# Decoder kernel: a prefetch hint at the loop heads, GpSimd's waits placed later in its chain, softplus work inside the attention tails, and the second attention's start in another order

## What is computed

```python
x = x + delta_rule(ln(x))      # L0_attn: 2 heads of 128, chunks of 64; decay per token and head
x = x + quantum_attn(ln(x), ctx)   # L0_xattn: 16 heads of 16, q, k, v through tanh(x W1 + b1) W2 + b2
x = x + moe4_top2(ln(x))       # L0_ffn: 4 experts of 512, layer norm inside, relu
x = x + latent_attn(ln(x))     # L1_attn: one latent of 128; k and v shared by 16 heads; causal
x = x + cross_attn(ln(x), ctx) # L1_xattn: 16 heads of 16, causal
x = x + moe8_top2(ln(x))       # L1_ffn: 8 experts of 128, gelu
```

```python
log_decay = -exp(A_log) * softplus(ln(x) @ W_alpha.T + dt_bias)
cum = cumsum(log_decay within a chunk);  L_mask = tril(exp(cum_i - cum_j))
```

## Time and profile before

| | before |
|---|---|
| PE busy | 4795.6 us (82%) |
| DVE busy | 4255.7 us (73%) |
| POOL busy | 3819.3 us (66%) |
| ACT busy | 2318.7 us (40%) |
| mean granted TensorE clock | 0.937 of 2.4 GHz |
| chain that ended last | PE 48%, DVE 22%, POOL 13%, issue 9%, ACT 6% |
| one round (start of the round's first L934 to the next one's: 2387.41 to 2729.33) | 341.9 us |

### The profile page before, as it was taken

The page is one execution under the profiler, slowest core; times in us unless marked ns, Lnnn a source line. Parts: engine busy times, 40 slices in busy tenths (PEclk is TensorE's granted clock), DMA queues, the critical chain, the costliest instruction groups (busy, mean ns, idle before and its releaser), DMA issues.

```text
span 5816.3 us, 105933 instructions
## 1 busy us (share of the span) xinstructions
PE 4795.6 (82%) x28362; PEld 3131.5 (54%) x28362; DVE 4255.7 (73%) x11558; ACT 2318.7 (40%) x4416; POOL 3819.3 (66%) x10625
## 2 busy tenths in 40 slices
PE   1068888988888888888988888898888889888888
PEld 0045654656555465655646565564656556465654
DVE  5867677777777677776767768777776777777677
ACT  0034344444434444343444434344443444443344
POOL 1157585775767677576766758676675867767585
PEclk7589999999999999999999999999999999999999
DMA  3000000000000000000000000000000000000000
GB/s 83 7 12 8 20 1 17 12 9 20 1 27 1 12 16 8 20 1 23 5 8 20 9 20 1 23 5 8 20 8 20 1 24 5 8 20 6 15 1 16
DMA packets 61954, 78.93 MB, mean 14 GB/s; under 512 B 11168, under 2 KB 53808, under 8 KB 61232
## 3 DMA queue, kind: packets, MB, share of 16 engines
q1 hardware_dynamic: 52784, 62.42, 3.2%
q10 hardware_dynamic: 8448, 8.39, 0.4%
HBM read 45.04 MB, written 8.46 MB: 9 GB/s over the span
## 4 chain that ended last, share of the span: by engine, by line
PE 48%; DVE 22%; POOL 13%; issue 9%; ACT 6%; POOLq 1%; SPq 1%; DMA 0%; DVEq 0%; ACTq 0%
PE bank L1161 7%; POOL acc_c L567 4%; PE bank L1066 4%; PE bank L1080 4%; PE bank L1194 4%; PE bank L1280 4%; POOL arena L567 3%; PE bank L1092 3%; PE bank L990 3%; PE bank L997 2%; PE bank L1114 2%; PE bank L1179 2%; ACT arena L761 1%; POOL sl_t L567 1%; DVE arena L1906 1%
## 5 line engine op out<-in xcount | busy, mean ns | idle before, releaser
L1765 DVE TENSOR_REDUCE smax<-bank 128x4 f32<-128x512 f32 x768 | 525.5, 684 | 146.9 <-PE bank L1072 97.5
L744 ACT ACTIVATE arena<-bank 128x512 f32<-128x512 f32 x768 | 454.9, 592 | 394.1 <-PE bank L1080 392.1
L1769 DVE TENSOR_TENSOR arena<-bank,smax 128x512 f32<-128x512 f32 x768 | 531.2, 692 | 26.4
L1080 PE MATMUL bank<-ident,arena 128*128 128x128 f32 x3072 | 492.0, 283 | 42.7 <-ACT arena L735 25.0
L1066 PE MATMUL bank<-arena 64*128 64x512 f32 x1536 | 451.0, 665 | 77.8 <-ACT arena L763 40.2
L1161 PE MATMUL bank<-w,arena 128*128 128x512 f32 x1024 | 485.6, 605 | 14.0 <-DVE arena L1717 14.0
L1092 PE MATMUL bank<-arena 128*32 128x128 f32 x6144 | 333.4, 289 | 192.3 <-ACT arena L748 192.3
L1080 PEld LDWEIGHTS bank<-ident,arena 128*128 128x128 f32 x3072 | 351.6, 143 | 241.7 <-ACT arena L737 82.3
L1194 PE MATMUL bank<-w,arena 128*128 128x256 f32 x2048 | 454.1, 380 | 13.9 <-ACT arena L798 13.9
L735 ACT ACTIVATE arena<-arena,rstd 128x512 f32<-128x512 f32 x512 | 368.1, 719 | 237.5 <-DVE arena L1769 232.9
L1194 PEld LDWEIGHTS bank<-w,arena 128*128 128x128 f32 x2048 | 387.8, 190 | 90.3 <-issue 23.0
(11 more groups left out here) (427 smaller groups left out, 11971.4 us busy)
## 6 DMA issues: line engine op xcount, KB each, us to landing
arena<-in_x_dram SPq DMA_DIRECT2D x35, 512.0 KB, 3.6
xn_next<-arena SPq DMA_DIRECT2D x17, 512.0 KB, 2.9
arena<-cum_dram SPq DMA_DIRECT2D x17, 512.0 KB, 3.7
arena<-in_ctx_dram SPq DMA_DIRECT2D x16, 512.0 KB, 3.5
out_dram<-arena ACTq DMA_DIRECT2D x16, 512.0 KB, 3.2
xn<-xn_next SPq DMA_DIRECT2D x15, 512.0 KB, 2.9
w<-in_L_ffn_w_dram SPq DMA_DIRECT2D x8, 512.0 KB
w<-in_L_ffn_w_dram SPq DMA_DIRECT2D x1, 1024.0 KB
```

The lines of the kernel that those rows point to most:

```text
L744: act.activation(PT[:, v % 2], bank[3 + v % 2][:, :].rearrange("p (h q) -> p h q", h=QH), ACT.Copy).then_inc(S["pt"], 1)
L1080: ins = tr(bank[3 + v % 2][:, j * P:(j + 1) * P], Ssb[:, v % 4, j, :], ident[:, :])
L1765: dve.tensor_reduce(smax[:, u, :], sc, AX, ALU.max).then_inc(S["s_max"], 1)
L1769: dve.tensor_tensor(Ssb[:, u % 4], sc, smax[:, u, :].unsqueeze(2).broadcast_to([P, QH, P]), ALU.subtract).then_inc(S["s_sub"], 1)
```

## The change

Five edits.

1. The loops of GpSimd, ScalarE, TensorE and VectorE are opened with `hint_back_edge=True`; a prefetch hint for the closing branch stands at each head. SyncE's loop is left as it is.
2. On GpSimd five of the first slice's 16 link groups stand ahead of the wait for `xn`. `ROUTER_LINKS` goes from 6 to 5, so the wait for `hl_mean`, the addition L594 and the wait for `g_w` come one group earlier. The wait for `x_norm` moves from ahead of the last slice's products to behind its eighth link group, and `CHAIN_READ` goes with it from 465 to 530.
3. On VectorE `decay_exponential` stands in attention 2 as parts 0 to 4 ahead of the third sequence's normalization and 5 to 9 ahead of the fourth's; before, parts 0 to 4 stood ahead of the fourth's and 5 to 9 behind the copy L1717 of the last norm.
4. At the start of attention 1 ScalarE writes the key masks in two halves (sequences 0 and 1, then 2 and 3), each of four instructions of 128x256 and not four of 128x512, and TensorE's third and fourth sequences wait for the second half alone.
5. There ScalarE's second half root (`half_rstd(3, 1, 2)`) stands ahead of the latent's copy, and VectorE's `beta_rows` (three small instructions) behind the keys, queries and values.

```diff
@@ -54,7 +54,7 @@
     MT=2, IT=2, V_psum=2, Vb=2, lev0=2, lev=12, inv_eye=2, W_psum=10, W=10, U_psum=10, U=10,
     T_psum=10, T=10, v1_psum=2, v1=2, c_psum=2, c_add=2, vnew_psum=2, vnew=2, oT_psum=2, oT=2, y0_psum=2,
-    h_psum=6, h_act=6, lat_psum=1, lat=1, q_psum=6, q=6, k_psum=5, k_rows=1, km=5, v_psum=5, v=6,
+    h_psum=6, h_act=6, lat_psum=1, lat=1, q_psum=6, q=6, k_psum=5, k_rows=1, km=6, v_psum=5, v=6,
     s_psum=48, s_max=48, s_sub=48, p_exp=48, t_psum=48, pt=48, pv=48, o_sb=12, otr_psum=12,
     o_rec=12, o_norm=12, attT_psum=12, attT=12, y_psum=6,
@@ -556,7 +556,7 @@
             first_squares(0, 0)
             decay_table(0, 0)
-            with pool.Fori(0, NIT) as it:
+            with nc.Fori(0, NIT, engines=[pool.engine], hint_back_edge=True) as it:
                 linked = [0]
@@ -583,10 +583,11 @@
                 pool.wait_ge(moved_now, nth(it, 16, 16))
                 pool.tensor_tensor(xres[:, :, :], xres[:, :, :], xn0[:, :, :], ALU.add).then_inc(S["xin_used"], 1)
+                chain_links(pool, link, 0, 0, 5)
                 pool.wait_ge(S["xn"], at(it, "xn", 4))
                 pool.tensor_tensor(xres[:, :, :], xres[:, :, :], bo_row[:, :].unsqueeze(1).broadcast_to([P, G, D]), ALU.add).then_inc(S["bias_res"], 1)
                 pool.wait_ge(ref_step, nth(it, REF_STEPS, REF_BEFORE + ROOT_STEPS))
-                chain_links(pool, link, 0, 0, 16)
+                chain_links(pool, link, 0, 5, 16)
                 chain_products(pool, link, src, 1)
                 chain_links(pool, link, 1, 0, ROUTER_LINKS)
@@ -598,10 +599,11 @@
                 chain_links(pool, link, 2, 0, 2)
                 chain_links(pool, link, 2, 2, 16)
+                chain_products(pool, link, src, 3)
+                chain_links(pool, link, 3, 0, 8)
                 pool.wait_ge(x_norm, nth(it, 1, 1, 2))
-                chain_products(pool, link, src, 3)
-                assert linked[0] == CHAIN_READ, linked[0]
-                chain_links(pool, link, 3, 0, 16)
+                assert linked[0] < CHAIN_READ, linked[0]
+                chain_links(pool, link, 3, 8, 16)
                 chain_end(pool, link)
                 assert linked[0] == CHAIN_STEPS, linked[0]
                 pool.wait_ge(chain_step, nth(it, CHAIN_STEPS, CHAIN_STEPS))
@@ -675,7 +677,7 @@
             beta_exp(0, 0)
             decay_exp(0, 0)
-            with act.Fori(0, NIT) as it:
+            with nc.Fori(0, NIT, engines=[act.engine], hint_back_edge=True) as it:
                 def second_rstd():
                     act.wait_ge(S["ln_mean"], at(it, "ln_mean", 1))
@@ -755,13 +757,22 @@
                 def key_masks(a_no, c, src, bias):
-                    act.wait_ge(S["k_psum"], at(it, "k_psum", KM_BEFORE[a_no] + c + 1))
+                    act.wait_ge(S["k_psum"], at(it, "k_psum", (0, 2, 3)[a_no] + c + 1))
                     for j in range(QH):
                         if bias:
                             ins = act.activation(KM[:, :, c, j, :], heads(src[:, :]), ACT.Identity, scale=halfmask[:, j:j + 1], bias=halfbias[:, j:j + 1])
                         else:
                             ins = act.activation(KM[:, :, c, j, :], heads(src[:, :]), ACT.Identity, scale=halfmask[:, j:j + 1])
                     ins.then_inc(S["km"], 1)
+
+                def latent_masks():
+
+                    act.wait_ge(S["k_psum"], at(it, "k_psum", 3))
+                    for m in range(2):
+                        two = slice(2 * m, 2 * m + 2)
+                        for j in range(QH):
+                            ins = act.activation(KM[:, two, 0, j, :], heads(bank[3][:, :])[:, two, :], ACT.Identity, scale=halfmask[:, j:j + 1])
+                        ins.then_inc(S["km"], 1)
                 half_rstd(0)
                 for n, k in enumerate((1, 2, 0)):
@@ -807,11 +818,10 @@
                 xT_copy(3)
-                half_rstd(3, 0, 1)
+                half_rstd(3)
                 act.wait_ge(S["lat_psum"], at(it, "lat_psum", 1))
                 act.activation(latT, bank[2][:, :], ACT.Copy).then_inc(S["lat"], 1)
-                half_rstd(3, 1, 2)
-                key_masks(1, 0, bank[3], False)
+                latent_masks()
                 attention(1)
@@ -922,7 +932,7 @@
             decay_rows(0, 3)
             decay_columns(0, 3)
-            with pe.Fori(0, NIT) as it:
+            with nc.Fori(0, NIT, engines=[pe.engine], hint_back_edge=True) as it:
                 def to_features(s):
                     if s == 0:
@@ -1058,7 +1068,7 @@
                         if u < QUADS and u % 2 == 0:
                             g, c = u // 4, (u % 4) // 2
-                            pe.wait_ge(S["km"], at(it, "km", KM_BEFORE[a_no] + min(c, chunks - 1) + 1))
+                            pe.wait_ge(S["km"], at(it, "km", KM_BEFORE[a_no] + (c if chunks > 1 else g // 2) + 1))
                             if u >= 4:
                                 pe.wait_ge(S["s_sub"], at(it, "s_sub", base + u - 2))
                             for v in (u, u + 1):
@@ -1641,7 +1651,7 @@
             decay_column(3)
             first_level(0, 0)
-            with dve.Fori(0, NIT) as it:
+            with nc.Fori(0, NIT, engines=[dve.engine], hint_back_edge=True) as it:
                 run["at"], run["n"], run["d"], run["before"], run["ref"], run["decay"] = it, 2, 1, REF_BEFORE, 0, 0
                 def wait(name, n):
@@ -1775,8 +1785,8 @@
                                 exact_difference(1)
                             if a_no == 1 and b == 3:
                                 exact_last(1)
-                            if a_no == 2 and b == 3:
-                                for part in range(5):
+                            if a_no == 2 and b >= 2:
+                                for part in range(5 * (b - 2), 5 * (b - 1)):
                                     decay_exponential(part)
                             wait("otr_psum", a_no * G + b + 1)
                             o = bank[7][:, :].rearrange("p (h d) -> p h d", d=2 * HD)
@@ -1940,7 +1950,6 @@
                 half_stats(3, 1, xres)
                 half_root(3, 0)
                 half_root(3, 1)
-                beta_rows(it, 1)
                 wait("v_psum", 3)
                 kv = bank[7][:, 0:G * 2 * HD].rearrange("p (g d) -> p g d", d=2 * HD)
                 dve.tensor_tensor(k_nat, kv[:, :, 0:HD].unsqueeze(2).broadcast_to([P, G, HPC, HD]),
@@ -1952,6 +1961,7 @@
                     for g in (2 * m, 2 * m + 1):
                         ins = dve.tensor_scalar(V2[:, g, :, 0:HD], kv[:, g, HD:2 * HD].unsqueeze(1).broadcast_to([P, NH, HD]), rstd[:, g:g + 1], None, ALU.mult)
                     ins.then_inc(S["v"], 1)
+                beta_rows(it, 1)
                 attention(1)
                 for m in range(2):
                     add_y(1, 6, m)
@@ -1970,8 +1980,6 @@
                 layer_norm(5, xres, lambda m: add_y(2, 8, m))
                 xT_copy(5)
-                for part in range(5, 10):
-                    decay_exponential(part)
                 wait("gl_psum", 1)
                 dve.tensor_copy(r_raw[:, :, :], bank[6][:, 0:G * E1].rearrange("p (g e) -> p g e", e=E1)).then_inc(S["g_ge"], 1)
                 wait("g_ge", 2)
@@ -2004,9 +2012,9 @@
 HIGH_BITS = -4096
 SPLIT = 4097.0
 MIX_FILL = 14
-ROUTER_LINKS = 6
+ROUTER_LINKS = 5
 REF_STEPS = 75
-CHAIN_READ = 465
+CHAIN_READ = 530
 PRODUCTS = 22
 LEVEL_PRODUCTS = (0, 4, 4, 8, 14, 19, 22)
 ROOT_STEPS = 41
@@ -2017,7 +2025,7 @@
 SET_POOL = 62
 SET_ROUTER = 14
 SET_DVE = 28
-KM_BEFORE = (0, 2, 3)
+KM_BEFORE = (0, 2, 4)
 S_BANKS = (0, 1, 2, 6)
 XT_BANKS = ((6, 7), (0, 1), (2, 6), (0, 1), (0, 1), (0, 1))
```

## The result

The changed kernel took 5644.8 us (median of four runs, 5637.7 to 5665.0) against 5820.7 us: a ratio of 0.9706, 95% interval 0.9682 to 0.9729, so 171 us faster by the ratio (158 to 185) and 176 by the medians. On another chip five more runs of it gave 5652.6 to 5685.0, median 5667.7, ratio 0.9737 (0.9714 to 0.9760). All nine have the median 5654.2, and I use that where an experiment is set against the changed kernel and no chip is named; one kernel's runs lie up to 47 us apart, so differences under some 20 us between changed kernels are not resolved by medians. The forecast was 5650, its range 5580 to 5735. The profiled execution took 5640.2 us, its span 5637.7, mean granted clock 0.950 (0.937 before).

What follows compares the result with a forecast made beforehand. GpSimd's chain bounds the tail of attention 2; elsewhere TensorE and VectorE take turns. Gains of 8.9 us a round (142 us over sixteen) plus 25.5 at the turns, 168 us off 5818.1, gave 5650; range 5580 to 5735.

Steps and rivals of the forecast that it cites:

- GpSimd's waits: GpSimd's chain: 33 early links put it 9.9 us ahead, `g_w` wait takes part back, `x_norm` wait goes; lead left 5.2 us.
- The margin: Tail of attention 2: `au` is written 9 us before VectorE asks for it at the end of L1769.
- Rival (b): Tail of attention 2: GpSimd's lead melts and VectorE waits at the third normalization; 5720 us, chance 0.09.
- The fourth normalization: VectorE, tail of attention 2: with `au` early and decay parts moved, it begins 4.4 us a round earlier.
- Parts 5 to 9 gone behind the last norm: VectorE between L1717 and L1976: L1976 comes 1.55 us a round earlier, not 3.7, since VectorE waits for L1248.
- the projection's clock: TensorE's last projection, L1114 in attention 2: higher clock after less idling gives 0 to 1.7 us; 0.85 a round taken.
- The loop's turn: TensorE at the loop's turn: of 4.2 us of gaps only 1.7 can be had, L1596 limiting; 25.5 us over 15 turns.
- The masks: Start of attention 1: TensorE waits for four masks of 128x256, 1.45 us instead of 2.42; 1.0 us a round earlier.
- the first part of the prediction: On what bounds the kernel: GpSimd's chain in the tail of attention 2; elsewhere TensorE and VectorE take turns.
- Where GpSimd meets VectorE: VectorE instructions held by GpSimd: 2.0 gained, 1.3 lost in router, 0.8 gained, 0.4 lost; net +1.1 us a round.
- The third term: Behind the last expert: the third slice's products end 5 us earlier, freeing about two held VectorE instructions, 0.8 us.
- the 0.4 us for the last slice's products: End of attention 1: products now lie beside VectorE instructions between two SBUF tiles, costing 0.4 us a round.

Runs made afterwards that it cites:

- The chain alone: Kernel before with only GpSimd's waits placed later and links moved ahead (no hints, masks and decay parts as before): 5714.4 us, ratio 0.9821.
- the kernel with all but the hints: Changed kernel with the four loops opened as before, without branch hints: 5705.1 us, ratio 0.9799 to the kernel before.
- the two hint experiments: Kernel before with only the four branch hints added, 5792.7 us; changed kernel without those four hints, 5705.1 us.
- the hints alone: Kernel before with nothing but the four branch hints on TensorE, VectorE, ScalarE and GpSimd: 5792.7 us, ratio 0.9954.
- the masks alone: Kernel before with the key masks in two halves, the earlier half root and the later beta rows: 5822.2 us, ratio 1.0006.

## Why the prediction was right

**GpSimd's waits: right, and the core of it.** 33 links came forward by 9.7 us (9.9 forecast), the wait for `g_w` costs 5.0 us a round (5 to 7), the one for `x_norm` is gone, and 11.9 us are left ahead of the addition of `bo_row` (some 10). The chain alone gave 106 of the 166 us.

**The margin: wrong in size, right in sign.** Counted from the start of `g_w`, `au` is written 145.4 us later, against 143.7 forecast and 162.1 before; that is 1.7 us of the error. The other 4.9 are VectorE's: it asks 147.6 us after `g_w` and not 152.5, because everything between became faster, of which the prediction had 1.4 us in its sum (0.8 to the keys' rows, 0.6 to q2) and none in the moment of asking. 9 us of margin were 2 in this round. In the 16 rounds of that execution they were 2.0 in seven, 3.4 to 3.9 in seven, and 9.4 and 8.7 in the two whose stage to q2 ran long at the lower clock, so that VectorE asked late. Rival (b) was nearer than the chance of 0.09 said.

**The fourth normalization: 3.7 us for 4.4.** The step failed at one instruction. It priced parts 5 to 9 at the 3.7 us that they took elsewhere, and did not look at what GpSimd does when it is done with the chain early: L501 (1.89 us) now meets them and holds L1496. That leaves TensorE 2.1 us a round of wait, where under 1 was forecast. Without L501 there the fourth normalization would have come at 2598.7 or a little later, better than forecast. The rounds bear that out: where L501 holds L1496, the stage from q2 to L1976 takes 52.6 to 53.6 us in the two profiles, and where it holds nothing 50.7 to 51.4; the forecast makes it 51.8. (The latter are the rounds in which VectorE asks late.)

**Parts 5 to 9 gone behind the last norm, and the projection's clock: 1.85 us for 2.4.** From the fourth normalization to L1976 lie 12.86 us, 14.71 before. VectorE now waits 2.44 us for L1258 there, as forecast, so L1258 sets it. The projection gave 0.70 us of clock, forecast 0.85.

**The loop's turn: right in place and in size, and partly taken back.** From the end of L923 (L913) to the second head's first transpose lie 5.29 us, against 6.97: 1.68 us, forecast 1.7. But the next 16 matmuls then ran slowly. In the kernel before they took 2.05 us:

```profile
2736.88 2.05 PE L990 MATMUL bank<-arena 128*128 128x128 f32 x16 [0.50 <-ACT arena L714]
```

The 3.49 us of now leave 0.2 us of the 1.7 in that round. The stage's mean shows 0.46 against the kernel before. Against the kernel with all but the hints it shows 1.4 to 1.6, though there this group is slow in only 4 turns of 15 (mean 2.51 us, 3.64 with the hints): the rest of the change lengthened that stage by 1.2 us. The medians of the two hint experiments show 27 and 51 us. Why the hints alone gave 27 us in the median and 7 in the profiled execution is open; the spread of one kernel goes with its clock (second chip: 5652.6 us at a mean granted clock of 0.948, 5685.0 at 0.939).

**The masks: 0.76 us a round for 1.0.** 28.0 against 40.2 us in 16 rounds. The first four of the eight take 1.57 us (2507.91 to 2509.48) and not the 1.45 of the prediction, which is half of what is missing. What the term left out lies behind the wait. Before, and in the changed kernel:

```profile
2579.32 2.08 PE L1066 MATMUL bank<-arena 64*128 64x512 f32 x4 [2.51 <-ACT arena L763]
```

```profile
2509.62 1.13 PE L1076 MATMUL bank<-arena 64*128 64x512 f32 x4 [1.75 <-ACT arena L774]
```

The first four score matmuls take over 1.3 us in 11 of 16 rounds before and in 13 with the old masks in the changed kernel, up to 2.08; behind the shorter wait they take 1.13 in all 16 rounds of the masks alone and in 14 and 10 of the changed kernel's two profiles. So this edit also kept the upper clock in most rounds, for up to 0.95 us each. Alone the masks gave nothing, since `au` was the bound; the condition that the term hung on was in the first part of the prediction and missing from this one.

**Where GpSimd meets VectorE: two of four terms seen at about their size.** L595 holds an instruction of the router for 1.4 us, and that stage grew by 1.3, the forecast's figure; the stage ahead of it shrank by 1.7 (2.0 forecast), and its small instructions are no longer beside products but beside links. The one that answers to L1699 of the earlier trace rows:

```profile
2424.73 0.22 DVE L1709 TENSOR_TENSOR parts<-parts 128x2 f32<-128x2 f32 x1
```
The third term, 0.8 behind the last expert, stands against 3.0 in the stage to the keys' rows. 0.7 us of that is TensorE's wait for an expert's z, which fell from 46.7 to 34.8 us (34.3 with the chain alone). The chain alone shows only 0.6 of the 3.0 in the mean, but 14 of its 16 rounds have 3.4 us or more at the lower clock there; its two others take 63.5 and 63.8 us, against 65.9 to 67.1 in such rounds of the kernel before. So the chain seems worth over 2 us there, most of it hidden by the clock when it stands alone. How much of it is contention is not settled, and the 0.4 us for the last slice's products can't be told from it.

**What the sum left out.** The time at the lower clock fell by 10 us a round in the first profile and by 5 in the second, most of it (6.8) in the tail whose idle time went. The forecast had 0.85 us for that, at one instruction. The sum agrees with the result because this, the 0.7 us behind `y_nat` and the stage to the keys stand against the head's loss, L501 and the masks; the total is nearer than its terms deserve.

## What to carry to other kernels

When work waits for a late producer, bring the producer forward first and then move the consumer's work: the same reordering cost 47 us with the producer late, and showed no cost with it early, where its own gain of some 20 us is not resolved. When a side engine gets ahead, look up what it does next and which instructions that will meet; and count a margin between two engines from one common event, with the consumer's own gain taken off, and in every round. Idle time of TensorE that is traded from one place to another can bring the lower clock to matmuls that ran at the upper one, so read the granted clock behind every wait that the change creates.

## What the runs showed of the hardware

- A branch hint at the loop's head took away both of TensorE's gaps at the turn (4.2 us) and five instruction transfers a turn, and cost nothing that shows.
- A small VectorE instruction with two inputs in SBUF that starts just behind a GpSimd one of 128x1024 ends with it, within 0.03 us in both cases looked at (1.82 us beside L501, 1.60 beside L595). The Trainium skill's "SBUF — State Buffer", "Who interferes with whom", says that a VectorE instruction with two SBUF inputs contends with a GpSimd one that reads SBUF, and, of VectorE's two-port modes, that whoever issues first has the shared ports for the whole instruction while the other blocks; the traces show such a block here.
- Spare matmuls in a gap raised the clock behind them both times: 3.49 to 2.05 us at the head, 3.62 to 1.89 at the tail. By the medians on one chip the first was worth 30 us, and the second nothing.
- Where TensorE's wait for the masks fell from 2.51 to 1.75 us, the granted clock mostly stayed up behind it: the four matmuls that follow took 1.13 us in 83 of the 96 rounds of six profiles, where in two profiles with the longer wait 24 of 32 rounds had 1.4 to 2.08.
